# Who issues the 64 stores of the turned masks: ACT at each half turn, or SyncE between its loads of the adjacency

## The reference

```
h = relu(layernorm(x));  Wh = h @ W
e = leaky_relu(Wh @ a1 + (Wh @ a2).T, 0.2)
x = x + relu(softmax(where(adj > 0, e, -9e15)) @ Wh)      # layer 0: attention
h = relu(layernorm(x))
node = h @ W1;  hw = einsum('nc,kcf->nkf', h, W2)
y = einsum('nk,nkf->nf', node, hw)
x = x + relu(adj @ y + node @ b)                          # layer 1: gather
```

## Time and profile before

| what | value |
|---|---|
| time, median of 3 runs | 1779.82 us (1768.06 to 1789.03) |
| profiled execution, its own time | 1774.92 us |
| its span, first to last instruction | 1773.3 us |
| PE busy / matmuls | 1709.6 us (96%) / 11311 |
| DVE busy | 1316.8 us (74%) |
| ACT busy | 1089.1 us (61%) |
| POOL busy | 640.0 us (36%) |
| DMA queue q1 (SP) | 356.58 MB, 73.1% of the 16 engines' span |
| DMA queue q10 (ACT) | 75.62 MB, 10.6% |
| mean granted TensorE clock | 0.99 |

### The profile page before, as it was taken

One profiled execution on the slowest core, in us unless ns is written; L12 is line 12 of the kernel. 1 busy time (PEld: TensorE's weight loads), 2 busy tenths in 40 slices (PEclk: granted clock), 3 DMA queues, 4 the chain that ended last, 5 costly groups with the idle time before them and its releaser, 6 DMA issues.

```text
span 1773.3 us, 36102 instructions
## 1 busy us (share of the span) xinstructions
PE 1709.6 (96%) x11311; PEld 1471.3 (83%) x11311; DVE 1316.8 (74%) x1775; ACT 1089.1 (61%) x1889; POOL 640.0 (36%) x522
## 2 busy tenths in 40 slices
PE   7999799999999999999999999999999999999998
PEld 4889688888888888888888888888777788888886
DVE  7778688899898898988888798888665543433534
ACT  4644476766666766667566667664556555555554
POOL 0000056455554655655545555655553300000000
PEclk9999899999999999999999999999999999999999
DMA  9999999999999999999999999996624444453430
GB/s 234 283 291 332 336 350 289 280 329 309 281 328 307 299 280 297 336 283 280 281 278 289 320 291 297 317 308 254 255 102 152 149 167 190 154 200 143 166 142 24
DMA packets 316753, 452.23 MB, mean 255 GB/s; under 512 B 21072, under 2 KB 291616, under 8 KB 298912
## 3 DMA queue, kind: packets, MB, share of 16 engines
q1 hardware_dynamic: 297664, 356.58, 73.1%
q10 hardware_dynamic: 12208, 75.62, 10.6%
q0 software_dynamic: 6832, 19.41, 3.4%
HBM read 364.46 MB, written 87.07 MB: 255 GB/s over the span
## 4 chain that ended last, share of the span: by engine, by line
PE 45%; SPq 15%; DMA 10%; DVE 10%; issue 9%; POOL 7%; ACT 2%; ACTq 0%; POOLq 0%; DVEq 0%
SPq L289 14%; PE ot_ps L800 14%; PE ot_ps L857 13%; PE mt_ps L857 13%; DMA keep_d<-keep 9%; DVE p_sb L989 6%; PE hw_ps L769 5%; POOL prod L399 5%; DVE mt L913 2%; DMA adj_sb<-in_adj_dram 1%; ACT prod L582 1%; POOL msg L402 1%; SPq L303 1%; DVE keep L970 1%; POOL msg L414 1%
## 5 line engine op out<-in xcount | busy, mean ns | idle before, releaser
L800 PEld LDWEIGHTS ot_ps<-wh_mask,p_sb 128*128 128x128 f32 x8192 | 947.2, 193 | 100.1 <-issue 86.2
L800 PE MATMUL ot_ps<-wh_mask,p_sb 128*128 (+1 forms) x8192 | 960.3, 277 | 35.2 <-DVE p_sb L989 21.8
L989 DVE SCALAR_TENSOR_TENSOR p_sb<-zb,qcol,mt 128x1024 f32<-128x1024 uint8 (+1 forms) x512 | 750.9, 1484 | 24.0 <-PE ot_ps L800 10.5
L399 POOL TENSOR_TENSOR prod<-prod 128x1024 f32<-128x1024 f32 (+2 forms) x192 | 383.9, 2000 | 499.4 <-ACT prod L582 441.1
L516 ACT ACTIVATE wh_mask<-adj_sb 128x2048 uint8<-128x2048 f32 x256 | 487.7, 1940 | 88.0 <-DMA adj_sb<-in_adj_dram 86.3
L1037 DVE CAST mask<-adj_sb 128x1024 fp32r<-128x1024 uint8 x272 | 204.0, 757 | 244.8 <-PE mt_ps L857 243.1
L609 ACT ACTIVATE mask<-adj_sb 128x1024 fp32r<-128x1024 uint8 x240 | 255.3, 1065 | 173.5 <-PE ot_ps L857 173.3
L582 ACT ACTIVATE prod<-hw_ps,node 128x128 f32<-128x128 f32 x1024 | 278.8, 384 | 116.0 <-PE hw_ps L769 115.0
L857 PE MATMUL mt_ps<-mask,msgs 128*128 128x512 f32 x1024 | 282.6, 398 | 2.1 <-DVE mask L1037 1.1
L857 PE MATMUL ot_ps<-mask,msgs 128*128 128x512 f32 x1024 | 274.8, 390 | 1.0 <-DVE mask L1037 0.5
L769 PE MATMUL hw_ps<-wcat,hT 128*128 128x512 f32 x512 | 242.4, 596 | 0.0
(11 more groups left out here) (108 smaller groups left out, 550.6 us busy)
## 6 DMA issues: line engine op xcount, KB each, us to landing
adj_sb<-in_adj_dram SPq DMA_DIRECT2D x1024, 256.0 KB, 7.6
maskT_d<-mt ACTq DMA_DIRECT2D x64, 1024.0 KB, 8.3
adj_sb<-maskT_d SPq DMA_DIRECT2D x32, 2048.0 KB, 7.8
keep_d<-keep POOLq DMA_DIRECT2D x64, 128.0 KB, 6.4
p_sb<-keep_d SPq DMA_DIRECT2D x4, 2048.0 KB, 12.1
msg_d<-msg POOLq DMA_DIRECT2D x56, 128.0 KB, 6.6
msgs<-msg_d SPq DMA_DIRECT2D x7, 1024.0 KB, 8.9
wh_mask<-in_x_dram SPq DMA_DIRECT2D x8, 512.0 KB, 9.5
```

Of the source, the lines that this page charges most:

```text
L399: pool.tensor_tensor(prod[:, 0:n, :], prod[:, 0:n, :], prod[:, n:2 * n, :], ALU.add)\
L800: ins = pe.matmul(ot_ps[h][:, (t - t0) * ROW:(t - t0 + 1) * ROW], p_sb[:, r, t * P:(t + 1) * P], rows, start=begin and t == t0, stop=end a ...
L989: dve.scalar_tensor_tensor(p_sb[:, r, :], zbf[:, bass.ds((ib % 2) * BLK, BLK)], qcol[:, bass.ds(tile + b_, 1)], mtb[:, p, k // 2, :, 2 * ( ...
```

## The change

The store is taken out of ACT's half turn and given to SP. SP's turn i loads buffers 0 and 1, then stores the masks of half turn (i - 2, p = 1); then it loads buffers 2 and 3, then stores those of (i - 1, p = 0). Ahead of each store SP waits for the four transposes of that half turn. Since SP's turn i runs ahead of the other engines, these are the masks that DVE has finished about then. SP's loop gets a second turn written out ahead of the loop of the first block (`two_first`), because the first stores don't exist yet, and the last three stores stand behind the loop. DVE's wait for `mt_stored` is as before.

```diff
-        def attention_loop(eng, turn, start_block=None, end_block=None, alone=False):
+        def attention_loop(eng, turn, start_block=None, end_block=None, alone=False, two_first=False):
...
-                with eng.Fori(1 if alone or not finish else 0, IT - 1) as jg:
+                if two_first and not finish:
+                    turn(ib * IT + 1, ib, 1, finish, False)
+                with eng.Fori(2 if two_first and not finish else 1 if alone or not finish else 0, IT - 1) as jg:
...
+            def store_masks(i, p):
+                sp.wait_ge(squared, A * (2 * i + p) + A)
+                sp.sem_inc(past_sp, 1)
+                sp.dma_start(maskT_d[bass.ds(2 * (i % IT) + p, 1), bass.ds(i // IT, 1), :, :]
+                             .rearrange("s i p w -> (s i p) w"),
+                             mt[:, p, :, :].rearrange("p c n -> p (c n)")).then_inc(mt_stored[p], 16)
...
                         if not (isinstance(i, int) and i == 0 and p == 0):
                             sp.wait_ge(adj_cast[q], i)
                             load_adj(ib, jg, p, h)
-
-            attention_loop(sp, turn)
+                    if p == 0 and not (isinstance(i, int) and i < 2):
+                        store_masks(i - 2, 1)
+                    if p == 1 and not (isinstance(i, int) and i < 1):
+                        store_masks(i - 1, 0)
+
+            attention_loop(sp, turn, two_first=True)
+            store_masks(NB * IT - 2, 1)
+            for p in range(2):
+                store_masks(NB * IT - 1, p)
...
-                        if k == 0:
-                            act.wait_ge(squared, A * n + A)
-                            act.dma_start(maskT_d[bass.ds(2 * jg + p, 1), bass.ds(ib, 1), :, :]
-                                          .rearrange("s i p w -> (s i p) w"),
-                                          mt[:, p, :, :].rearrange("p c n -> p (c n)")).then_inc(mt_stored[p], 16)
```

## The result

| | before | after |
|---|---|---|
| time, median of 4 runs each | 1773.94 us (1767.46 to 1789.03) | 1869.81 us (1862.62 to 1880.03) |
| profiled execution, its own time | 1774.92 us | 1862.62 us |
| its span | 1773.3 us | 1861.0 us |
| start of half turn 8 (block 1) on PE | 203.3 | 201.7 |
| half turns 8 to 59 ("the stage") | 974.0 us, 18.73 each | 1062.4 us, 20.43 each |

What follows compares the result with a forecast made beforehand. PE was taken to set the pace from block 1 on, with the DMA engines full beside it. Terms of 3.3 + 2.4 + 12.9 + 4.3 + 8 + 5 = 36 us on 1779.8 gave 1816, forecast as 1815, range 1776 to 1870.

Steps and rivals of the forecast that it cites:

- What bounds the kernel: From block 1 on PE sets the pace, DMA engines full beside it; PE gains nothing from a freer ACT.
- What goes and what comes: ACT's 22 us of store issues go, costed at nothing; SP gains 0.6 us each, 38 in all, hidden by its waits.
- What moves: Store goes behind eight loads in SP's queue, landing about when they do; half turn 25 just comes out even.
- It is paid once for each rise: DVE and PE lose one us per further us SP falls behind, once per rise: 3.3, 2.4, 12.9 and 4.3 us.
- wobble: Small lateness in each of the 50 other half turns: 0.1 us each, 5 us in all, between 0 and 15.
- Block 0: First block, half turn 2: DVE some 16 us late, between 4 and 16 paid, taken as 8 us.
- The last three stores: Stores ahead of SP's mask loads for the gather: nothing added, up to 3 us.
- Late in every half turn: Rival: store lands 2.8 us later than counted, recurring over 56 half turns, 95 us, 1875 us; chance 0.13.
- Nothing changes: Rival: store lands as fast as before or SP never falls behind, 1780 us; chance 0.17.
- Not slower, 1768: Rival: loads no longer overtaken in block 0 and half turn 49's pause gone, together 11.5 us won; chance 0.1.
- What would show it: Signs in the later trace: landings 20 us or more after transposes, DVE newly waiting, most in block 0 and 820 to 1000 us.
- the lag: Time from ACT's store to the last issue of SP's eight loads, 8.6 us in half turn 25; forecast no longer above 10.

Runs made afterwards that it cites:

- e1_ahead: The changed kernel with SP issuing each store between the loads of its two buffers, ahead of its wait for the late cast; 1789.13 us, ratio 1.0029.
- e11_after_twelve: The changed kernel with each store placed behind four loads of the next buffer as well as the eight loads; 1961.37 us, ratio 1.1013.
- e3_half: The changed kernel with SP storing only half turns with p = 0, and ACT those with p = 1 as before; 1888.69 us, ratio 1.0599.
- e12_ahead_later_need_again: The changed kernel with stores between the two buffers' loads and DVE asking one k later, repeated with more executions; 1793.56 us, ratio 1.0031.

## Why the prediction was right or wrong

**What bounds the kernel**: right as to PE, and a freer ACT gave nothing: in e1_ahead ACT issues no store, and the time is as before. That the DMA engines were full beside it the share of 1.09 does not show: it is 1.07 after the change at 280 GB/s.

**What goes and what comes**: right, and near nothing. SP's issue is 0.36 us where I took 0.6, and its wait for `squared` is met within the loop.

**What moves** is where the sum went wrong, in two steps. The first is "loads plus store are through at about the same time as the loads were: the store lands at about 537.5". It lands 2.3 to 3.8 us after the last of the eight loads (2.75 in the median), not with them; the two runs with fewer bytes, 0.3 and 1.5 us, put this down to the store's own megabyte. With that, half turn 25 doesn't come out even. By the measured offsets the store lands 10.0 + 10.2 us after PE's start at 520.4 (the store of the earlier trace rows, less 0.6), so at 540.6; DVE wants it at 534.7 and has 2.5 us of idle time. It is 5.9 late and pays 3.4.

The second step, the one that decided the size, is "It is paid once for each rise". Its reason, "when PE is later, the casts and ACT are later by as much, and SP is no longer behind them", was half seen. SP is indeed no longer behind: its loads start 3.5 us after PE's start in the median and in none of 50 half turns later than 4 us, where they came 6.2 us after it in the mean before, in 20 of 50 later than 4. So the rises that I added up (n = 15 and one taken like it, 48, 51 to 55; 22.9 us of the 36) did not take place. But a later PE makes the casts, the eight loads and with them the **store** later by as much: lateness moves on with the loop and comes back two half turns later. Paid every second half turn of 52, 26 x 3.4 = 88 us, where the trace lost 88.4. That it fits so closely is luck, since the 2.5 us are of one half turn; the kind of sum is right. e11_after_twelve shows the same rate at another place.

What each half turn pays on its own I had put at 0.1 us ("wobble"); it is 88.4 / 52 = 1.7. And the spread of 1793 to 1845 is not what the ends given add up to (4 to 16, 0 to 15, and 3 for the last stores: 1806 to 1836).

**Block 0** was put at 8 us and cost nothing here (203.3 before, 201.7 after); as that point lies anywhere from 188.5 to 232.8 in the other profiles, one profile can't settle it. **The last three stores**: 596.0 and 596.9 us from half turn 60 to the end, nothing, as costed.

**The rivals.** "Late in every half turn" had the right price, 95 us, from the right cause, a full store behind the loads. Its reason for 0.13 was the objection "a later PE leaves a shorter queue": true (SP waits for casts now), but a shorter queue doesn't bring the store forward, since the eight loads in front of it wait for the cast. And its loop closes in two half turns, not one, as e3_half shows. Its 1.7 us for a half turn is right by luck: 2.8 us late, 2.8 more for the store and 2.5 of slack leave 3.1, and it takes the loop of two half turns to halve that to 1.6. "Nothing changes" is what e1_ahead measures: that would have been right with the store one buffer earlier. "Not slower, 1768" showed in no run: no ratio is below 1.

**What would show it**: ACT's queue is without stores (q10 8.5 MB instead of 75.6), DVE newly waits, PE waits for `p_sb`, the gather is unchanged, and the last of the eight loads is issued at most 9.9 us (8.1 in the median) after the moment at which ACT stored before, so the lag stays under 10. From the end of the transposes to the landing it is 570.2 - 543.6 = 26.5 us in half turn 25, over the 20 that I named. The waits are not most in block 0 and between 820 and 1000, but everywhere, which I had named as the sign that the lag isn't paid once.

By the rule of the Trainium skill that several issuing engines save only issue time ("DMA: Bandwidth & Descriptors", section "Issuing engines are not separate DMA queues") nothing would have changed. For the queue alone the runs come near to it (e1_ahead); what the rule doesn't cover is the place in the issuing engine's order, and that was nearly the whole cost.

## What to carry to other kernels

When a transfer is moved to another engine's order, ask what the instruction ahead of it waits for. If that goes back to the engine which the transfer's landing releases, you have closed a loop: add up one round of it, divide by the half turns that it spans (the number of buffers), and compare with the period; whatever is over is paid in every round, however full the other engines are. If the round was under it, the move was free here to within 1%, and so was the queue (e1_ahead and e12_ahead_later_need_again).

## What was not expected of the hardware

A queue of its own is worth little to a store of 1 MB here: 8.3 us to landing at the start of the half turn and 9.0 late in it, against 9.8 to 10.3 (page medians) in SP's queue in e1_ahead and the changed kernel. From the share of 84.8% in the earlier trace rows I had expected more. And an eighth of the bytes still takes 7.5 us; it lands right behind the loads ahead of it.

Short pauses of PE can cost more than their length. The granted clock of PE before, in and behind the two pauses of 2.25 and 1.44 us in half turn 23 (stretch, length, PE busy, clock, DMA share, GB/s):

```profile
505.00:511.00 6.00, 4.13 (x34) 1.00 1.09 272
511.00:517.00 6.00, 4.18 (x23) 0.65 1.13 243
517.00:523.00 6.00, 6.00 (x45) 0.78 1.08 294
523.00:530.00 7.00, 7.00 (x44) 1.00 1.08 325
```

At 0.65 and 0.78 part of each stretch ran at 1.2 GHz, the rest at 2.4. 14 of the 52 half turns show a mean clock of 0.86 to 0.93; PE idles 2.4 to 3.9 us in each of them. Seven others with as much (half turns 10, 11, 13, 29, 33, 39 and 49, 2.4 to 4.4 us) stay at 1.00. PE is busy 19.8 to 21.4 us in these 14, and about 18.3 in the others, 28 us more in all, against 5 in two such half turns before the change: here lie the 23 us that it is busy longer in the stage. So about a quarter of the loss is not the wait for the stores itself but goes with the lower clock behind the waits.
